# A DLRM tower on one core: first two tables picked in float32, identity turned early, first ids on another queue, eight row banks

## What is computed

```
e = stack([tbl_f[ids[:, f]] for f in range(32)], axis=1)      # 512 x 32 x 128
dot = einsum('bnd,bmd->bnm', e, e)
z = dot[:, iu, ju]                                            # upper triangle, 496
h = concatenate([z, dense_ctx], axis=1)                       # 512 x 512
h = maximum(h @ W_top1 + b_top1, 0.0)                         # 512 x 512
h = maximum(h @ W_top2 + b_top2, 0.0)                         # 512 x 256
y = h @ W_top3                                                # 512 x 1
```

## Time and profile before

| | us |
|---|---|
| median of 3 runs | 150.77 |
| lowest, highest | 150.52, 151.89 |
| the profiled execution | 150.31 |
| its span | 148.5 |

### The profile page before, as it was taken

How to read it: one execution, slowest core, us unless ns; L and a number is a source line. 1 busy time by engine, 2 the same in 40 slices (tenths; PEclk the granted TensorE clock), 3 DMA queues, 4 the chain that set the end, 5 groups by cost and what they waited for, 6 DMA issues and landing times.

```text
span 148.5 us, 2544 instructions
## 1 busy us (share of the span) xinstructions
PE 119.0 (80%) x1008; PEld 96.8 (65%) x1008; DVE 81.2 (55%) x80; ACT 68.6 (46%) x109; POOL 76.0 (51%) x80
## 2 busy tenths in 40 slices
PE   0195998789999989769599764487499989799993
PEld 0174776476777776545488564276499979699971
DVE  1599997899999999676993000020113041313300
ACT  3359806989998974069961051012024040300032
POOL 3777885747788777848777567506301700000000
PEclk9999999999999999999779969559869999999999
DMA  2797776557647868882212112205425733042000
GB/s 64 187 338 240 283 214 194 124 160 216 206 121 176 272 226 246 233 288 53 53 35 53 53 33 57 53 2 126 114 63 130 188 99 73 4 141 71 4 0 1
DMA packets 10990, 19.29 MB, mean 130 GB/s; under 512 B 2385, under 2 KB 7377, under 8 KB 10978
## 3 DMA queue, kind: packets, MB, share of 16 engines
q1 hardware_dynamic: 8290, 14.01, 32.0%
q0 software_dynamic: 2304, 4.72, 11.6%
q10 hardware_dynamic: 384, 0.39, 0.8%
HBM read 17.02 MB, written 2.13 MB: 129 GB/s over the span
## 4 chain that ended last, share of the span: by engine, by line
PE 65%; issue 14%; DVE 12%; another core or an unknown queue 4%; ACT 2%; DMA 1%; DVEq 0%
PE two_ps L479 16%; PE two_ps L481 13%; DVE onehot L290 9%; PE two_ps L519 8%; PE two_ps L528 8%; PE free_ps L519 7%; PE turn_ps L495 5%; PE free_ps L539 3%; DVE low L275 3%; PE two_ps L539 2%; ACT emb L353 2%; PE two_ps L544 1%; DMA id_sb<-row_ids 1%; PE turn_ps L528 1%
## 5 line engine op out<-in xcount | busy, mean ns | idle before, releaser
L266 POOL DMA_INDIRECT rows<-tables,row_no x72 | 75.1, 1044 | 42.3 <-issue 19.5
L479 PE MATMUL two_ps<-onehot,high 128*128 128x512 f32 x118 | 50.7, 430 | 15.5 <-DVE low L275 6.9
L290 DVE TENSOR_TENSOR onehot<-pick_id,free_ps 128x1536 fp32r<-128x1536 int16 (+2 forms) x30 | 53.1, 1800 | 4.2 <-DMA pick_id<-pick_ids 2.1
L481 PE MATMUL two_ps<-onehot,low 128*128 128x512 f32 x118 | 48.4, 410 | 0.0
L479 PEld LDWEIGHTS two_ps<-onehot,high 128*128 128x128 f32 x118 | 23.5, 199 | 27.0 <-issue 21.1
L481 PEld LDWEIGHTS two_ps<-onehot,low 128*128 128x128 f32 x118 | 23.5, 199 | 4.4
L275 DVE TENSOR_TENSOR low<-home,high 128x1024 fp32r<-128x1024 f32 (+2 forms) x17 | 18.3, 1076 | 3.0 <-ACT high L353 1.6
L519 PE MATMUL two_ps<-emb 128*64 128x64 f32 x240 | 12.8, 263 | 7.8 <-issue 6.8
L353 ACT ACTIVATE high<-home 128x1024 fp32r<-128x1024 f32 (+2 forms) x17 | 15.8, 941 | 4.9 <-DMA home<-picked 4.2
L373 ACT ACTIVATE away<-pick_id,less_row 128x512 f16<-128x512 int16 x25 | 16.7, 715 | 1.4 <-DMA pick_id<-pick_ids 1.4
L179 DVE COPY home<-free_ps 128x512 f32<-128x512 f32 x4 | 2.8, 692 | 26.4 <-remote 24.1
(11 more groups left out here) (32 smaller groups left out, 46.4 us busy)
## 6 DMA issues: line engine op xcount, KB each, us to landing
home<-picked SPq DMA_DIRECT2D x10, 512.0 KB
home<-picked SPq DMA_DIRECT2D x3, 640.0 KB
pick_id<-pick_ids SPq DMA_DIRECT2D x14, 128.0 KB
dot_out<-home SPq DMA_DIRECT2D x14, 128.0 KB, 2.5
w_sb<-w SPq DMA_DIRECT2D x3, 512.0 KB
rows<-tables,row_no POOLq DMA_INDIRECT x72
pairs<-dot_out SPq DMA_DIRECT2D x14, 64.0 KB, 2.0
home<-picked SPq DMA_DIRECT2D x4, 128.0 KB, 3.9
```

What stands on the lines that cost most here:

```text
L266: pool.indirect_dma_start(rows[:, k % ROWS_HELD, i, :], None, tables, bass.IndirectOffsetOnAxis(ap=row_no[:, c:c + 1], axis=0)).then_inc(r ...
L290: dve.tensor_tensor(onehot[:, c % HOT:c % HOT + n, :], ids, own, ALU.is_equal).then_inc(onehot_dve, n)
L479: pe.matmul(out, high[:, at, D * k:D * (k + 1)], onehot[:, c % HOT, :], start=(k == 0), stop=False)
L481: pe.matmul(out, low[:, at, D * k:D * (k + 1)], onehot[:, c % HOT, :], start=False, stop=(k == KR[t] - 1)).then_inc(picked_done, 1)
```

## The change

- `WHOLE = 2`: tables 0 and 1 are not split. PE multiplies the table's own chunk by the one-hot read as float32, one float32 matmul a chunk. DVE's `low` and ACT's `high` of these tables are gone, with ACT's copies of the four pieces. PE waits for the pieces and for table 1 itself. `low` and `high` of tables 3 and 4 no longer wait for picks, and the loads of tables 3 and 4 wait for all picks of tables 0 and 1 (they took the place of a wait for parts).
- `WARM = 14`: after the identity is ready PE turns it 14 times into `turn_ps[0]`, which nothing reads.
- Ids 0 and 1 are loaded from ACT's queue, at the head of its program; SP keeps the others.
- `ROWS_HELD = 8` banks. Up to bank 13 POOL waits as before (`AHEAD = 4`: bank k waits for the turn of bank k - 4). Banks 14 to 18 wait for 11 turned banks and bank 19 for 12.

The diff:

```diff
--- before.py
+++ after.py
@@ -21,6 +21,8 @@
 PIECE = 2
 PIECES0 = KR[0] // PIECE
 
+WHOLE = 2
+
 BY_ACT = [0, 2, 2, 2, 1, 2, 2, 2, 2, 1, 2, 2, 2, 3]
 
 TWOS = -(-PICK // 2)
@@ -39,7 +41,10 @@
 TILE0 = [sum(TILES[:k]) for k in range(NB + 1)]
 
 TURNED = PICK - 1
-TABLES_HELD, IDS_HELD, HOT, AWAY, ROWS_HELD = 3, 4, 16, 6, 4
+TABLES_HELD, IDS_HELD, HOT, AWAY, ROWS_HELD = 3, 4, 16, 6, 8
+
+AHEAD = 4
+WARM = 14
 
 BATCH = 4
 
@@ -163,7 +168,7 @@
 
         def parts_made(t):
 
-            return PIECES0 + t
+            return t - WHOLE + 1
 
         def by_dve(t):
 
@@ -178,6 +183,10 @@
             at = GRP // 4 * (grp % 2) + GRP // 8 * j
             return copy(dot_sb[:, grp // 2 % 2, :, at:at + GRP // 8],
                         dot_ps[grp % 2][j][:, :].rearrange("p (g c) -> p c g", c=2 * F))
+
+        def ids_load(queue, t):
+            queue.dma_start(pick_id[:, t % IDS_HELD, :],
+                            pick_ids[t:t + 1, :].broadcast_to([P, B])).then_inc(pick_ids_in[t], 16)
 
         def dots_store(queue, r, s):
             queue.dma_start(dot_out[r][s, 0:F * F, :].rearrange("(a j) g -> a j g", j=F),
@@ -205,28 +214,27 @@
 
         @block.sync
         def _(sp):
-            def ids_load(t):
-                if t >= IDS_HELD:
-                    sp.wait_ge(onehot_dve, by_dve(t - IDS_HELD + 1))
-                    sp.wait_ge(away_ready, ACT0[t - IDS_HELD + 1])
-                sp.dma_start(pick_id[:, t % IDS_HELD, :],
-                             pick_ids[t:t + 1, :].broadcast_to([P, B])).then_inc(pick_ids_in[t], 16)
-
             def table_load(t):
-                if t >= TABLES_HELD:
+                if TABLES_HELD <= t < TABLES_HELD + WHOLE:
+                    sp.wait_ge(picked_done, CHUNK0[t - TABLES_HELD + 1])
+                elif t >= TABLES_HELD:
                     sp.wait_ge(low_ready, parts_made(t - TABLES_HELD))
                 sp.dma_start(table[:, t % TABLES_HELD, 0:width(t)],
                              picked[P * CHUNK0[t]:P * CHUNK0[t + 1], :].rearrange("(p k) d -> p (k d)", k=KR[t])
                              ).then_inc(table_in[t], 16)
 
             sp.dma_start(id_sb[:, :, :], row_ids).then_inc(row_ids_in, 16)
-            ids_load(0)
+
             first = picked[0:P * KR[0], :].rearrange("(p k) d -> p (k d)", k=KR[0])
             n = PIECE * D
             for j in range(PIECES0):
                 sp.dma_start(table[:, 0, n * j:n * (j + 1)], first[:, n * j:n * (j + 1)]).then_inc(piece_in[j], 16)
             for t in range(1, PICK):
-                ids_load(t)
+                if t >= IDS_HELD:
+                    sp.wait_ge(onehot_dve, by_dve(t - IDS_HELD + 1))
+                    sp.wait_ge(away_ready, ACT0[t - IDS_HELD + 1])
+                if t > 1:
+                    ids_load(sp, t)
                 table_load(t)
             for r in range(BLOCKS):
                 sp.dma_start(dot_out[r][:, F * F:F * F + CTX, :], context[r]).then_inc(context_in, 16)
@@ -259,8 +267,8 @@
                                base=0, pattern=[[-1, P]], channel_multiplier=1).then_inc(ident_ready, 1)
             pool.wait_ge(row_no_ready, 1)
             for k in range(NB):
-                if k >= ROWS_HELD:
-                    pool.wait_ge(turned, k - ROWS_HELD + 1)
+                if k >= AHEAD:
+                    pool.wait_ge(turned, min(k - AHEAD + 1, max(PICK - 3, k - ROWS_HELD + 1)))
                 for i in range(TILES[k]):
                     c = TILE0[k] + i
                     pool.indirect_dma_start(
@@ -270,9 +278,9 @@
 
         @block.vector
         def _(dve):
-            def split_low(t, a, b):
-                at = t % TABLES_HELD
-                dve.tensor_tensor(low[:, at, a:b], table[:, at, a:b], high[:, at, a:b],
+            def split_low(t):
+                at, n = t % TABLES_HELD, width(t)
+                dve.tensor_tensor(low[:, at, 0:n], table[:, at, 0:n], high[:, at, 0:n],
                                   ALU.subtract).then_inc(low_ready, 1)
 
             def make_onehots(t, k0, k1):
@@ -310,13 +318,12 @@
             dve.wait_ge(pick_ids_in[0], 16)
             for j in range(PIECES0):
                 make_onehots(0, PIECE * j, min(PIECE * (j + 1), KR[0] - BY_ACT[0]))
-                dve.wait_ge(high_ready, j + 1)
-                split_low(0, PIECE * D * j, PIECE * D * (j + 1))
             for t in range(1, PICK):
-                dve.wait_ge(high_ready, parts_made(t))
-                if t >= TABLES_HELD:
-                    dve.wait_ge(picked_done, CHUNK0[t - TABLES_HELD + 1])
-                split_low(t, 0, width(t))
+                if t >= WHOLE:
+                    dve.wait_ge(high_ready, parts_made(t))
+                    if t >= TABLES_HELD + WHOLE:
+                        dve.wait_ge(picked_done, CHUNK0[t - TABLES_HELD + 1])
+                    split_low(t)
                 dve.wait_ge(pick_ids_in[t], 16)
                 make_onehots(t, 0, KR[t] - BY_ACT[t])
 
@@ -407,13 +414,10 @@
                     act.wait_ge(dots_stored[grp // 2 - 2], 64)
                 copy_dots(copy, grp, 0).then_inc(dots_act, 1)
 
-            for j in range(PIECES0):
-                act.wait_ge(piece_in[j], 16)
-                n = PIECE * D
-                copy(high[:, 0, n * j:n * (j + 1)], table[:, 0, n * j:n * (j + 1)]).then_inc(high_ready, 1)
+            ids_load(act, 0)
+            ids_load(act, 1)
             act.wait_ge(less_row_ready, len(STEPS))
             make_away(1)
-            split_high(1)
             make_away(2)
             split_high(2)
             for t in range(PICK):
@@ -464,18 +468,24 @@
             def pick(t):
                 if t >= 4:
                     pe.wait_ge(pick_emb_ready, t // 2 - 1)
-                if t:
+                if t >= WHOLE:
                     pe.wait_ge(low_ready, parts_made(t))
+                elif t:
+                    pe.wait_ge(table_in[t], 16)
                 at, out = t % TABLES_HELD, two_ps[t // 2 % 2][:, t % 2, :]
                 own = KR[t] - BY_ACT[t]
                 for k in range(KR[t]):
                     c = CHUNK0[t] + k
                     if t == 0 and k % PIECE == 0:
-                        pe.wait_ge(low_ready, k // PIECE + 1)
+                        pe.wait_ge(piece_in[k // PIECE], 16)
                     if k < own:
                         pe.wait_ge(onehot_dve, by_dve(t) + k + 1)
                     else:
                         pe.wait_ge(onehot_act, ACT0[t] + k - own + 1)
+                    if t < WHOLE:
+                        pe.matmul(out, table[:, at, D * k:D * (k + 1)], onehot[:, c % HOT, :].bitcast(f32),
+                                  start=(k == 0), stop=(k == KR[t] - 1)).then_inc(picked_done, 1)
+                        continue
                     pe.matmul(out, high[:, at, D * k:D * (k + 1)], onehot[:, c % HOT, :],
                               start=(k == 0), stop=False)
                     pe.matmul(out, low[:, at, D * k:D * (k + 1)], onehot[:, c % HOT, :],
@@ -546,6 +556,9 @@
                 return last
 
             pe.wait_ge(ident_ready, 2)
+
+            for i in range(WARM):
+                pe.transpose(turn_ps[0][:, 0:P], ident[:, :], ident[:, :])
             for t in range(PICK):
                 pick(t)
                 if t:
```

## The result

| | before | after |
|---|---|---|
| median us (runs) | 151.33 (4) | 159.12 (4) |
| lowest to highest | 150.52 to 152.08 | 158.64 to 159.75 |
| the profiled execution, its span | 150.31, 148.5 | 159.75, 157.9 |

The ratio is 1.052 [1.044, 1.060], with its 95% interval in brackets: slower, outside the range that was given. A ratio here leaves out the executions that stood over 1.5% above the fastest of the same kernel, so it can differ from the ratio of two medians. The layers behind the dots take what they took (157.9 - 122.74 = 35.2 us against 148.5 - 113.65 = 34.9), so the 9 us lie ahead of them.

A forecast was written before the change was run, and what follows sets the result against it. It took VectorE, with TensorE close behind, to bound the pick stage, and POOL's gathers to stall the dots; -1.6 us in the picks became +0.9 at the dots' end, so 150.31 + 0.9 = 151.2 us, range 148.1 to 153.3.

The forecast's parts named there:

- the price of the gathers in one piece: Dots stage: all 16 last gathers lie over the dots and slow them; stage ends at 114.5 against 113.65, +0.9 us.
- The wait before the dots: Between last pick and dots: wait kept as before, so dots start at 86.70 - 1.6 = 85.1 us.
- The pace: Dots under POOL's gathers: about 3 records a microsecond pass, 109 of 384 done by 103.5 us.
- The tail: Dots after POOL's last gather: TensorE still slowed for 1.3 us, until 103.5, then 38 ns a record.
- Table 4: Pick stage: its load, issued at 19.9 when table 1 is picked, arrives at 23.8; `low` starts at 24.9 against 26.51.
- The picks: Rest of the pick stage: of 2.2 + 0.5 us taken from VectorE's work 1.6 survive, -1.6 us.
- The float32 price: Picks of tables 0 and 1: 0.865 us a chunk at 2.4 GHz, 1.7 at 1.2 GHz, against 0.47 now.
- The clock: Start of the picks: 14 transposes have TensorE's clock already high, so table 1 ends at 19.9 us.
- rival B: Start of the picks: clock stays low, table 1 ends at 22.0, kernel slower at 153.3 us; chance 0.20.
- Ids on ScalarE's queue: Kernel start: ids 0 issue sooner, VectorE starts at 4.8; -0.5 us, bounds 0 and -2.0.
- Rival A: Dots stage: the stalls are not the gathers' doing, so 1.6 us survive, 149.2 us; chance 0.28.
- Rival C: Dots stage: banks do nothing, clock cold, gathers and stalls not linked; 151.3 us, no change; chance 0.10.

The follow-up runs named there:

- e11: Kernel before with all 72 gathers by index made plain transfers from POOL's queue (other rows come): 129.01 us, 0.8505 of the kernel before.
- e13: Kernel before with only the eight banks and their new wait, in a set at 150 us: 157.55 us, ratio 1.0376.
- e14: Changed kernel with POOL waiting ahead of bank 16 for the turns of banks 0 to 12, set at 150 us: 158.55 us, ratio 1.0362.
- e10: Changed kernel with four banks, their old wait and all ids on SyncE's queue: 149.44 us, 1.0002 of the kernel before.
- e9: Kernel before with eight banks and its own plain wait (bank k for the turn of bank k - 8): 155.84 us, ratio 1.0448.
- e12: Kernel before with bank 16 waiting for the dots of the first six groups: 152.75 us, ratio 1.0189.
- e5: Changed kernel as it is, run again in a set at 129 us: 130.00 us, 1.0036 of the kernel before.
- e6: Kernel before as it is, run again for its trace in a set at 129 us: 129.11 us, ratio 1.0012.
- e1: Changed kernel with four banks and their old wait, set at 129 us: 130.60 us, 1.0125 of the kernel before.
- e4: Changed kernel with banks 14 to 19 filled by plain transfers (other rows come), set at 129 us: 129.61 us, 0.9926 of the kernel before.
- e3: Changed kernel with POOL waiting ahead of bank 16 for the turns of banks 0 to 12, set at 129 us: 130.41 us, too wide for a ratio.
- e15: Kernel before with ids 0 and 1 alone moved to ScalarE's queue, set at 129 us: 130.81 us, ratio 1.0115.
- e2: Kernel before with only the eight banks and their new wait, in a set at 129 us: 128.73 us, ratio 0.9987.
- sets 2, 3 and 5: Three sets of runs on one and the same chip; the kernel before took 129.08, 149.52 and 128.91 us there.
- e7: Changed kernel with WARM = 0 (no turns of the identity), set at 129 us: 131.13 us, 1.0130 of the kernel before.
- e8: Kernel before with eight banks, early turns and ids 0 and 1 on ScalarE's queue, parts kept, set at 129 us: 130.45 us, ratio 1.0150.
- e16: Changed kernel, eight banks, with all ids back on SyncE's queue, set at 129 us: median 130.65 us, too wide for a ratio.

## Why the prediction was wrong

**The step that failed** is the price of the gathers in one piece: "about 3 a microsecond pass ... until 1.3 us after the last gather", and with it "the dots start at 85.1". The mechanism was right (0.62 of the chances lay on it, and e11 shows it), but it was priced only where I had seen it, as a slower stream of dots, and the stage's total was taken to move by +0.9. It moved by +9.1. Of the 8.2 us between, 5.9 lie behind the last pick (+8.4 measured, +2.5 foretold) and 2.3 before it (+0.7 and -1.6).

- *The wait before the dots.* I carried the 3.4 us from the last pick to the dots over unchanged. They held 2.3 us from the last pick to ScalarE's copy, where e11 has 0.2, and the copy came inside POOL's wait of 2.08 us, the very wait that the banks remove. The row stood in my list and I counted it only as POOL's gain. With no pause it took 17.4 us in the changed kernel. But a pause isn't needed for the signal: e13 and e14 have none there either, their copies came after 1.8 and 0.2 us, and their delay came in the dots instead. What decides between the two places no run shows; the stage ends at about the same time.
- *The pace.* 3 records a microsecond was read from 90.0 to 97.17, behind POOL's pause and on past its last gather at 95.6. Under longer rows of gathers without a pause e13 and e14 show about 1, that is some 20 records in as many microseconds where my sum let 46 through in 15.
- *The tail.* The dots run freely 1.0 and 1.6 us after POOL stops in the kernel before, behind stretches of 4.7 and 9.7 us without a pause. They do so 2.0 us after one of 12.2 (e10), 1.6 after 15.8 (e9), 2.9 after 19.7 (e12), and 4.0, 4.0 and 4.5 after 27, 33 and 38 us (e13, e14 and the changed kernel, 105.36 to 109.87). That the tail grows with the length of the stretch is a reading of these eight; no run varies the length alone.
- *Table 4.* Foretold: its `low` at 24.9. It came at 29.71. At the cold clock my sum had 27.0; the rest is the late signal again: table 1 is picked by 22.4 and its load goes out at 24.98 (loads of tables 3 and 4 now wait for `picked_done`, TensorE's signal, where they had waited for VectorE's). In e14, with the full clock and table 1 picked by 20.5, it still was 29.22. With no late signals it is 27.54 (e5) against 24.76 in the kernel before (e6), so at the late clock the new start itself costs 2.8 us, and the turns behind the last pick show it: 79.94 against 77.12. At the full clock it costs 0.3 (25.07 in e1 and e4, turns at 77.5). My baseline of 26.51 already held a late signal, which flattered the change.
- *The picks.* -1.6 foretold, +0.7 measured. The float32 price was right: 0.865 us a chunk against 0.87 (e1).
- *The clock.* Rise 4.4 us after the first pick as before, so rival B's case: table 1 ends at 22.4 (22.0 foretold). The Trainium skill (TensorE: Matmul & The Clock Gate, Part 4) says that transposes don't engage the full clock. The changed kernel and e5 agree with it. e1, e4 and e14 don't: there nothing but 14 turns (1.71 to 4.96) went before, and the first pick already ran at 2.4 GHz; in e4 and e14 the recorded clock rises at 5.23 and 5.57, ahead of it. The same page (Part 1) calls the rise variable from run to run, which the two runs of one program, e3 and e14, bear out (9.84 and 5.57).
- *Ids on ScalarE's queue.* -0.5 was taken, and bounds of 0 and -2.0. I priced what the moved transfer gains and not what it takes: the row ids, now beside two broadcasts of ids, landed 1.6 us later, and POOL's row of 72 gathers starts from them. Alone it costs 1.15% (e15). "Nothing waited for the later banks" holds in the kernel before at 150 us and not once the dots are quick: then bank 18 is waited for (1.50 us in e6).

Rival A (the stalls are not the gathers' doing) is refuted by e11 and by e12. Rival C's "banks do nothing" holds only in the sets at 129 us (e2), and B's sum was too small by the same terms as the forecast's.

**What stays open.** What sets off the late signals: the same program shows none in a set at 129 us, gathers and all, and on the same chip (sets 2, 3 and 5). No run here tells what differs. Nor does one tell what in a gather by index does it, the index, the longer work of POOL or the scattered rows.

## What to carry to other kernels

When an engine's wait is removed, ask what went on elsewhere during that wait, and not only what its owner gains. A stall read from coincidence should be priced at its worst place (every signal of the stalled engine, all along the overlap) as one end of the range, and a pace taken beside short stretches of the cause is no price for a long one. An experiment that was to pause an engine has to be looked at for the pause (e14 had none). A transfer put on another queue isn't free for those it used to follow: look who waits for them.

## What the runs showed of the hardware

- While POOL gathers by index, in the sets at 150 us, TensorE's signals can arrive late, by up to 17.4 us (the changed kernel), and its short matmuls go down to about one record a microsecond (e13, e14). It is 15% of the kernel (e11: 22 of 151 us). Plain transfers from the same queue didn't do it in the one set where they were tried.
- A kernel can have two levels of time, 129 and 150 us, that hold for a whole set of runs, on one and the same chip; the late signals are the difference that the traces show.
- A gather by index of 128 rows keeps POOL 0.94 us and the next starts 1.25 us after it; a plain transfer of the same size keeps it 0.53 us (e11).
- The clock can be full after 14 transposes alone (e4, e14: it rises at 5.23 and 5.57, before the first pick), and can rise 4.4 us into the picks with the same start (the changed kernel).
- A float32 matmul of 128 x 512 takes 0.87 us at 2.4 GHz, against 0.47 for two float32r ones.
- With two broadcasts of ids on a second queue a transfer on the first landed 1.1 to 2.1 us later (row numbers at 2.76 in the kernel before, 3.86 to 4.86 in e1, e3, e4, e5, e7, e8, e14, e15 and the changed kernel, and at 2.75 again in e10 and e16).
